# The causal mask of the row maxima in one wave of 64 rows, two queries to a row, in a transformer block on one core

## The reference

```python
q, k = _apply_rope(q, cos, sin), _apply_rope(k, cos, sin)
scores = jnp.einsum('bhqd,bhkd->bhqk', q, k) / jnp.sqrt(jnp.asarray(hd, x.dtype))
scores = jnp.where(causal, scores, jnp.asarray(-jnp.inf, x.dtype))
y = jnp.einsum('bhqk,bhkd->bhqd', jax.nn.softmax(scores, axis=-1), v)
...                                                  # + gating * adapter attention
x = x + _layernorm(attn(_layernorm(x)))
x = x + _layernorm(ffn(_layernorm(x)))
```

## Time and profile before

| | |
|---|---|
| time, median of 3 runs | 1148.98 us (1147.29 to 1150.64) |
| span of the profiled execution, first to last instruction | 1144.4 us |
| TensorE busy, whole span | 1080.7 us (94%), 7020 matmuls |
| VectorE busy | 697.3 us (61%) |
| ScalarE busy | 502.8 us (44%) |
| GpSimd busy | 264.8 us (23%) |
| granted TensorE clock, mean | 0.974 |
| mask matmuls (line 1029) | 1024, mean 228 ns, busy 83.9 us |

### The profile page before, as it was taken

The page is one execution under the profiler, slowest core; times in us unless marked ns, Lnnn a source line. Parts: engine busy times, 40 slices in busy tenths (PEclk is TensorE's granted clock), DMA queues, the critical chain, the costliest instruction groups (busy, mean ns, idle before and its releaser), DMA issues. The chain is left out here.

```text
span 1144.4 us, 18108 instructions
## 1 busy us (share of the span) xinstructions
PE 1080.7 (94%) x7020; PEld 726.5 (63%) x7020; DVE 697.3 (61%) x976; ACT 502.8 (44%) x1054; POOL 264.8 (23%) x260
## 2 busy tenths in 40 slices
PE   5999999988999999999999989879999999999997
PEld 4778778643444444444444444667888887887885
DVE  5747646887788888888888763764435224324114
ACT  3223242345777777777777755033321121111111
POOL 6715436401311111111111242440001001001001
PEclk9999999878999999999999999899999999999999
DMA  7456777850444444445443426544313003001001
GB/s 250 133 146 184 164 177 172 157 109 21 93 92 87 91 89 89 93 90 94 87 87 94 145 70 193 184 143 139 106 38 111 1 1 111 1 1 53 21 1 38
DMA packets 93949, 113.08 MB, mean 99 GB/s; under 512 B 26536, under 2 KB 54824, under 8 KB 93864
## 3 DMA queue, kind: packets, MB, share of 16 engines
q1 hardware_dynamic: 91656, 107.81, 36.9%
q10 hardware_dynamic: 2208, 4.11, 2.2%
HBM read 68.82 MB, written 42.21 MB: 97 GB/s over the span
## 5 line engine op out<-in xcount | busy, mean ns | idle before, releaser
L908 ACT ACTIVATE prob<-ps_s 128x512 f32<-128x512 f32 (+3 forms) x768 | 329.3, 493 | 147.6 <-PE ps_s L1059 142.9
L932 DVE TENSOR_REDUCE neg<-ps_m 128x2 f32<-128x1024 f32 (+2 forms) x224 | 250.4, 1145 | 64.1 <-PE ps_m L1024 31.2
L1059 PE MATMUL ps_s<-q_op,k_op 50*128 50x512 f32 (+2 forms) x768 | 211.5, 438 | 5.9 <-ACT prob L908 1.6
L1059 PEld LDWEIGHTS ps_s<-q_op,k_op 50*128 50x128 f32 x768 | 101.8, 189 | 122.4 <-ACT prob L908 102.0
L1024 PE MATMUL ps_m<-k_op,q_op 48*128 48x512 f32 (+2 forms) x768 | 162.5, 416 | 7.6 <-DVE neg L932 6.2
L864 POOL TENSOR_SCALAR_AFFINE_SELECT prob<-prob 128x512 f32<-128x512 f32 x128 | 83.9, 657 | 369.9 <-ACT prob L908 369.8
L1075 PE MATMUL ps_y<-prob,vg 128*17 128x512 f32 (+3 forms) x1536 | 160.6, 499 | 7.3 <-ACT y_sb L887 7.3
L1685 DVE TENSOR_TENSOR hf<-sl,ps_u 128x512 f32<-128x512 f32 (+1 forms) x44 | 30.2, 686 | 170.0 <-PE ps_u L79 149.3
L1024 PEld LDWEIGHTS ps_m<-k_op,q_op 48*128 48x128 f32 x768 | 84.2, 194 | 40.9 <-DVE neg L932 15.5
L1784 PE MATMUL ps_d<-w_high,wp_high 128*128 128x512 f32 (+1 forms) x328 | 107.4, 390 | 0.0
L932 DVE TENSOR_REDUCE neg_far<-ps_m 128x4 f32<-128x512 f32 (+2 forms) x96 | 97.3, 1043 | 13.1 <-PE ps_m L1029 12.3
(11 more groups left out here) (197 smaller groups left out, 1683.6 us busy)
## 6 DMA issues: line engine op xcount, KB each, us to landing
y_heads<-y_sb SPq DMA_DIRECT2D x32, 256.0 KB, 4.2
raw<-in_w_ffn SPq DMA_DIRECT2D x31, 256.0 KB, 3.3
k_op<-k_parts SPq DMA_DIRECT2D x28, 256.0 KB, 4.6
q_op<-q_parts SPq DMA_DIRECT2D x56, 128.0 KB, 5.1
v_groups<-v_out SPq DMA_DIRECT2D x16, 272.0 KB, 4.1
q_parts<-part_h SPq DMA_DIRECT2D x16, 256.0 KB, 3.0
q_parts<-part_l SPq DMA_DIRECT2D x16, 256.0 KB, 2.9
k_parts<-part_h SPq DMA_DIRECT2D x16, 256.0 KB, 2.9
```

What stands on the lines that cost most here:

```text
L908: act.activation(prob[:, v % NPROB, h, unit_cols(u)], ps_s[:, y % NS, unit_cols(u)], ACT.Exp, scale=D ** -0.5).then_inc(s_exp, 1)
L932: nc.vector.tensor_reduce(to[:, :, pairs[0]:pairs[-1] + 1, i - TT * c], scores, axis=AX.X, op=ALU.max, negate=True).then_inc(a_read, 1)
L1059: nc.tensor.matmul(ps_s[:, y % NS, lo:BLK], k_op[buf][r, pair, j * P:(j + 1) * P], q_op[buf][r, c, pair, lo:BLK], start=True, stop=True)\
```

## The change

The mask of 128 queries is made with 64 rows instead of two times 64. Row r of the new tile `above_h` stands for the queries 2r and 2r + 1 and holds, at key k, 0 for k up to 2r, -2^43 at k = 2r + 1, and -2^126 beyond. The tile `pick_h` holds in row r 1.0 at query 2r and 2^-83 at query 2r + 1. Query 2r gets the row as it is. Query 2r + 1 gets it times 2^-83: -2^-40, as good as nothing, at its own key, and -2^43 beyond. So one wave masks what took two.

`above_h` holds the triangle twice, side by side. In a short chunk one matmul for each `s` then adds the mask to both pairs: 256 columns in, and an output of two runs of 128 columns, one in each pair's part of the bank. For that the bank's accumulation is opened once, by the first pair's scores (`start=x == 0`), and the mask comes behind both pairs' scores. GpSimd makes the tiles with the same six instructions; two selects and a memset change their width, and one more wait stands between the two rounds of selects.

```diff
-MASKED = -3.0e38
+FIRST, REST, FAINT = -2.0 ** 43, -2.0 ** 126, 2.0 ** -83
...
-    for half in range(2):
-        pool.affine_select(out=ident_h[0:64, half], in_=ident_h[0:64, half], compare_op=ALU.not_equal,
-                           fill=1.0, base=64 * half, pattern=[[-1, P]], channel_multiplier=1).then_inc(mask_const, 1)
-        pool.affine_select(out=causal_h[0:64, half], in_=causal_h[0:64, half], compare_op=ALU.is_ge,
-                           fill=MASKED, base=64 * half, pattern=[[-1, P]], channel_multiplier=1)\
-            .then_inc(mask_const, 1)
-    wait_alone(pool, passed, mask_const, 6)
+    for odd in range(2):
+        pool.affine_select(out=pick_h[0:64], in_=pick_h[0:64], compare_op=ALU.not_equal, fill=(1.0, FAINT)[odd],
+                           base=odd, pattern=[[-1, P]], channel_multiplier=2).then_inc(mask_const, 1)
+        pool.affine_select(out=above_h[0:64], in_=above_h[0:64], compare_op=ALU.is_ge, fill=(FIRST, REST)[odd],
+                           base=odd, pattern=[[0, HG // 2], [-1, P]], channel_multiplier=2).then_inc(mask_const, 1)
+        wait_alone(pool, passed, mask_const, 4 + 2 * odd)
...
+            masked = lo + keys == (i + 1) * P
             for x, pair in enumerate(pairs):
-                base = x * wide
-                diag = base + i * P - lo
-                masks = (0, 1) if lo + keys == (i + 1) * P else ()
                 for s in range(2):
                     r = slice(64 * s, 64 * s + KQ)
-                    last = nc.tensor.matmul(ps_m[:, g % 2, s, base:base + wide], q_op[buf][r, c, pair, (i - TT * c) * P:(i - TT * c + 1) * P],
-                                            k_op[buf][r, pair, lo:lo + wide], start=True, stop=not masks)
-                for half in masks:
-                    for s in range(2):
-                        r = slice(64 * s, 64 * s + 64)
-                        last = nc.tensor.matmul(ps_m[:, g % 2, s, diag:diag + P], ident_h[r, half], causal_h[r, half],
-                                                start=False, stop=half == 1)
+                    last = nc.tensor.matmul(ps_m[:, g % 2, s, x * wide:(x + 1) * wide],
+                                            q_op[buf][r, c, pair, (i - TT * c) * P:(i - TT * c + 1) * P],
+                                            k_op[buf][r, pair, lo:lo + wide], start=x == 0,
+                                            stop=not masked and x == len(pairs) - 1)
+            for s in range(2 if masked else 0):
+                r = slice(64 * s, 64 * s + 64)
+                diag = ps_m[:, g % 2, s, 0:len(pairs) * wide].rearrange("p (x n) -> p x n", n=wide)[:, :, keys - P:keys]
+                last = nc.tensor.matmul(diag, pick_h[r], above_h[r, 0:len(pairs)], start=False, stop=True)
             last.then_inc(a_ps, 1)
...
-        masks_of = [place.put(name, [P, 2, P], BF16) for name in ("ident_h", "causal_h")]
+        masks_of = [place.put(name, shape, BF16) for name, shape in (("pick_h", [P, P]), ("above_h", [P, HG // 2, P]))]
```

More of the change, by code:

```diff
@@ L103, in put, with build_masks @@
         return tensor
-def build_masks(pool, passed, ident_h, causal_h, mask_const):
-    pool.memset(ident_h[:], 0.0).then_inc(mask_const, 1)
-    pool.memset(causal_h[:], 0.0).then_inc(mask_const, 1)
+def build_masks(pool, passed, pick_h, above_h, mask_const):
+    pool.memset(pick_h[:], 0.0).then_inc(mask_const, 1)
+    pool.memset(above_h[:], 0.0).then_inc(mask_const, 1)
     wait_alone(pool, passed, mask_const, 2)
-    for half in range(2):
-        pool.affine_select(out=ident_h[0:64, half], in_=ident_h[0:64, half], compare_op=ALU.not_equal,
-                           fill=1.0, base=64 * half, pattern=[[-1, P]], channel_multiplier=1).then_inc(mask_const, 1)
-        pool.affine_select(out=causal_h[0:64, half], in_=causal_h[0:64, half], compare_op=ALU.is_ge,
-                           fill=MASKED, base=64 * half, pattern=[[-1, P]], channel_multiplier=1)\
-            .then_inc(mask_const, 1)
-    wait_alone(pool, passed, mask_const, 6)
+    for odd in range(2):
[4 more added lines that the diff above has]
+        wait_alone(pool, passed, mask_const, 4 + 2 * odd)
 def ones_below(pool, passed, k_buf, op_const):
@@ L153, in stage_inputs @@
         aT_ps aT_ready ya_ps ya_ready*2 ya_stored*2""")
-    ident_h, causal_h = masks_of
+    pick_h, above_h = masks_of
     q_op, k_op, vg = operands
@@ L213, in _ @@
         sp.wait_ge(mask_const, 6)
-        for half in (ident_h, causal_h):
+        for half in (pick_h, above_h):
             sp.dma_start(half[64:P], half[0:64]).then_inc(mask_in, 16)
@@ L284, in _ @@
                 .then_inc(w_low_pool, 1)
-        build_masks(pool, passed, ident_h, causal_h, mask_const)
+        build_masks(pool, passed, pick_h, above_h, mask_const)
         ones_below(pool, passed, k_op[0], op_const[0])
@@ L1189, in __init__ @@
         for at, count in ((start["q_op0"], 4), (start["x"], 4), (start["wqk_h"], 4), (start["wqk_l"], 4), (late.at, 4),
-                          (start["ident_h"], 2), (start["a_raw"], 8), (start["heads"], 1), (x1_at, 2)):
+                          (start["pick_h"], 2), (start["a_raw"], 8), (start["heads"], 1), (x1_at, 2)):
             place = Map(nc, at)
```

## The result

| | before | after |
|---|---|---|
| time, median of the first 4 runs each | 1148.26 us (1147.29 to 1150.64) | 1137.32 us (1136.98 to 1138.82) |
| ratio, 95% interval | | 0.990 (0.987 to 0.993) |
| span of the profiled execution | 1144.4 us | 1137.0 us (time 1138.82) |
| TensorE busy, matmuls | 1080.7 us, 7020 | 1073.1 us, 6380 |
| granted TensorE clock, mean | 0.974 | 0.969 |

The sign and the place are as predicted; the size is not. Two questions follow: how much of the 10.9 us is the change, and which terms of the sum were mis-sized.

The account below looks back on a forecast made before the run. The prediction took attention as bound by TensorE and ScalarE waiting for each other in turn; 0.40 us a group over 13.3 groups (5.3 us) plus 0.5 in the opening took 1149.0 to 1143.2 us, range 1139.5 to 1147.5.

Parts of the forecast that it names:

- What bounds, and where: Attention: TensorE and ScalarE wait for each other in turn; only savings ahead of ScalarE's six gaps shorten a group.
- The single pieces: Single-pair chunks in attention: one of two equal mask waves goes, saving 0.05 us for each of four on the chain.
- The 384 piece ahead of 420.87: Single-pair chunk of 384 columns ahead of ScalarE's first gap (0.18 us); counted on the chain at 0.05 us.
- The near short chunks: Two two-pair chunks between the scores of 424.85 and 426.32, ahead of the exponentials at 426.88; 0.10 us saved each.
- the sum for the chunk after: Short chunk after the change: 0.22 us bare wave plus 0.30 with its mask, 0.52 against 0.61 before; 0.10 taken.
- the gain passes each gap: At ScalarE's gaps in a group: each saving is smaller than the idle time there, such as 0.20 against 0.41 us.
- The far short chunks: The group's other two short chunks, under 11 exponentials without a gap, where ScalarE sets the pace: worth nothing.
- The sum: Attention: 0.40 us a group times 13.3 groups is 5.3 us, plus 0.5 for the opening: 5.8 us (2.4 to 10.1).
- groups at 27.4 us: Sign in the changed profile: attention groups take 27.4 us instead of 27.8.
- The opening: Attention from 194.8 to 276 us, 2.7 groups, VectorE mostly the pace: half taken, 0.5 us (0 to 1.3).
- The base: Whole kernel: the saving is taken off the median of 1149.0 us, 4.6 above the profile's span of 1144.4.
- The clock rival: Attention: less TensorE work drops the clock; some 3 us per 10.2 us fall, 1152 for three falls; chance 0.08.

Follow-up runs that it names:

- changed_again: The changed kernel run once more without an edit, beside the kernel before on the same chip; 1141.35 us, ratio 0.991.
- before_again: The kernel before run once more without an edit, with a profile; ratio 1.001 against itself, profile span 1150.2 us.
- merged_two_halves: Against the kernel before: old mask tiles and columns, but short chunks put both pairs' scores first, then one mask matmul per half for both pairs; 1143.98 us, ratio 0.995.
- mask_twice: Against the changed kernel: each mask wave is issued twice, so mask columns are as many as before; 1144.88 us, ratio 0.996 to the kernel before.
- singles_as_before: Against the changed kernel: the eight single-pair chunks of a group get two mask waves of 128 columns again; 1142.40 us, ratio 0.993 to the kernel before.
- short_chunk_ahead: Against the changed kernel: the first near short chunk moved ahead of the product that waits for the output copy; 1148.24 us, ratio 0.997 to the kernel before.
- no_masks: Against the changed kernel: the whole causal mask of the maxima is left out; 1163.80 us, ratio 1.013 to the kernel before.

## Why the prediction was right in part

**What bounds, and where.** Right in the main. The gain lies in attention, in the stretches ahead of ScalarE's gaps, and the stages before 194 us and behind 690 us took no part in it: against the profile of before, TensorE's work in that of changed_again, which has no fall of the clock from 290 to 636 us, is 0.3 us late at 194 us, 1.6 early at 287, 7.8 at 645, and 6.4 at the end, since it has one more fall of the clock at 659 us. (The first profile after is 1.2 us ahead at 194 us, which the change doesn't explain.)

**The single pieces.** Forecast 0.05 for each of four on the chain, 0.20; measured 0.15. Three are right. The 384 piece ahead of 420.87 gives nothing (I is the same with and without it).

**The near short chunks.** The failing step is the sum for the chunk after, 0.22 us for the bare wave and 0.30 for the wave with the mask behind it. The 0.22 is the distance from a score of line 1059 to the wave behind it. From one wave of maxima to the next it is 0.12 us in the first chunk (392.76 to 392.88) and 0.20 in the second (393.04 to 393.24), and the wave with the mask takes 0.16 and 0.17 (to 393.04 and 393.41). So a chunk is 0.28 or 0.37 us, not 0.52, and saves 0.24, not 0.10 and not the 0.17 of the upper end. Of the 0.48 us of both, 0.25 reach the group. The argument that the gain passes each gap compared 0.20 with the gap of 0.41 us; the real 0.48 closes that gap. And it looked at ScalarE's gaps alone and left out the other rule of the kernel, by which a score waits for an exponential: beyond some 0.25 us this wait is late next. By these two errors against each other 0.20 became 0.25; that this term came out near its forecast is luck.

**The far short chunks.** "Worth nothing" is the step that failed outright: 0.12 us a group. A run of exponentials in one line of the view was read as ScalarE setting the pace, but it held idle times of up to 0.11 us, and at one place its pieces were 0.38 us apart where 0.27 is possible.

**The sum.** 0.51 instead of 0.40 us a group, times 13.3: 6.8 instead of 5.3 us. (The sign of groups at 27.4 us came true all the same, as the base was read as 27.8 and is 27.87.) The opening gave 1.1 to 2.3 us from 194 to 276 us in the three profiles of the changed kernel, against the first one of before, not 0.5; against before_again, whose half clock lasted longer, it would be 4 to 5 more. With 1.4, that of the first profile after, that makes 8.2 us, within the prediction's own ends (2.4 to 10.1), and near the 8.7 of the many executions; as the opening's term depends on which profile of before is taken, this agreement is partly luck. Taken off the median of the first runs it would have been 1140.8 us. The remaining 3.5 us down to 1137.3, with which the time leaves the range, belong to the first four executions: of the 19 later ones only two are as short. Why these four were quick isn't known.

**The base.** The saving was taken off a median of 1149.0 us. Later medians are 1148.6 to 1150.6, so the base was right; it was the profile that was quick: its span and the 1.8 us that lie around it in the profile after make 1146.2 us, some 2 to 4 us under these. The expectation of before_again, that a quick profile puts the forecast too high, doesn't follow, as the saving was taken off the median and not off the profile.

**The clock rival.** It had 0.08 and came true in some executions. The lowest mean clock among the 103 executions of the kernel before and the 22 of the three kernels that keep two mask waves, or as many columns, on the single pieces (merged_two_halves, mask_twice, singles_as_before) is 0.965. Of the 73 of the kernels with one wave there 19 are below 0.965 (seven of them of short_chunk_ahead), down to 0.951, and the four of no_masks are at 0.921 to 0.937. In the 17 executions of the changed kernel at 0.969 and above the median is 1139.47 us; in the 85 of before, 1149.25. So by this bound, which was set after the fact, the change gives 9.8 us where the clock holds, and about 1 us of it is lost to the clock on average. The rival's price for a fall, 3 us for 10.2 us at half clock, holds: falls of 3.4 and 6.8 us cost a group 0.9 and 2.1 us (28.22 and 29.43 against 27.36). Its 1152 for three falls is what three executions show (1150.7 to 1152.1), but by luck: the profiled one of them has four falls between 440 and 680 us, 44 us in all, of which one is 30.7 us, and the base without falls is 1139.5, not 1143.2.

**What stays open.** Why the clock falls in some executions of a kernel and not in others isn't shown. Between 8.2 us by the groups and the opening, and 9.8 at a clock of 0.969 and above, 1.6 us have no place in the traces. The lengths of the falls in the opening differ from execution to execution in both kernels, and the profiles are too few to say whether the change moves them. What an order with full single masks and merged short chunks is worth against the changed kernel (singles_as_before: 0.15 us a group slower, never below 0.969 in five executions, 1142.40 us) isn't settled either; five executions are few. No kernel was found that beats the changed one.

## What to carry to other kernels

A row of back-to-back instructions without idle time proves nothing by itself: look at it piece by piece, and compare the distance of their starts with the shortest distance that the same shape reaches elsewhere, since a wait of less than their overlap leaves no gap. When a piece in front of a bottleneck gets shorter, look for every rule by which the next piece waits, not only for the gap that was there. And taking work away from TensorE can cost its clock: with all masks gone the groups were the shortest where the clock held, and the kernel the slowest.

## What the runs showed of the hardware that was not expected

- Score waves of 256 columns follow each other after 0.12 us when nothing stands between or ahead of them, after 0.20 us where a mask wave stands ahead of the first (393.04 to 393.24), and after 0.22 to 0.30 us with two mask waves of 128 columns between (425.19 to 425.41, 425.41 to 425.72). The 0.12 is seen best in no_masks, on TensorE's timeline, where four such waves (eight matmuls) take 0.48 us up to the next score:

```profile
370.01 0.64 PE L1021 MATMUL ps_m<-k_op,q_op 48*128 48x256 f32 x8
370.49 0.87 PE L1057 MATMUL ps_s<-q_op,k_op 50*128 50x512 f32 x2
```

- A mask wave of 256 columns whose result goes to two runs of 128 columns is cheaper than two waves of 128: 0.65 us against 0.75 for the two near short chunks.
- Exponentials of 256 columns last 0.38 us each and follow one another after 0.27 us.
- Without the masks TensorE was busy 25.79 of 27.03 us in a clean group (95%; 97% before), and still the clock went back to 0.50 again and again: 0.87 on the mean from 290 to 640 us.
